# Products without a reader on TensorE, and the reversed scan's parts at other steps

## The reference, cut to what matters

```python
x = _L0_conv_ref(x, ...)             # bidirectional selective scan (Mamba) over 2 images of 256 x 48 x 48
x = x + _L1_conv_ref(_gn(x), ...)    # linear attention block
t = _to_tokens(x)
t = t + _L2_attn_ref(_ln_t(t), ...)  # softmax attention
t = t + _L2_ffn_ref(_ln_t(t), ...)   # graph-gated experts
t = t + _L3_attn_ref(_ln_t(t), ...)  # att = sigmoid((n q) n^T);  att n
t = t + _L3_ffn_ref(_ln_t(t), ...)   # routed experts
...
def step(h, xs):                     # the scan, once forward and once reversed
    d_t, B_t, C_t, u_t = xs
    h = jnp.exp(d_t[..., None] * A) * h + (d_t * u_t)[..., None] * B_t[:, None, :]
    return (h, jnp.einsum('bdn,bn->bd', h, C_t))
# y * silu(z), then out_proj;  _ln_t: (v - mean) / sqrt(var + eps) over the channels
```

## Time and profile before

| | |
|---|---|
| median of 3 runs | 5890.46 us (5889.35 to 5890.49) |
| the profiled execution: its own time, its span | 5906.89 us, 5905.1 us |
| mean granted TensorE clock | 0.917 |
| busy: PE, DVE, ACT, POOL | 4882.1, 3428.7, 2082.3, 2321.0 us |

### The profile page before, as it was taken

How to read it: one execution, slowest core, us unless ns; L and a number is a source line. 1 busy time by engine, 2 the same in 40 slices (tenths; PEclk the granted TensorE clock), 3 DMA queues, 4 the chain that set the end, 5 groups by cost and what they waited for, 6 DMA issues and landing times. The chain is left out here.

```text
span 5905.1 us, 54130 instructions
## 1 busy us (share of the span) xinstructions
PE 4882.1 (83%) x15186; PEld 2726.7 (46%) x15187; DVE 3428.7 (58%) x4954; ACT 2082.3 (35%) x3362; POOL 2321.0 (39%) x2102
## 2 busy tenths in 40 slices
PE   5877888987778886998997876473999899997797
PEld 3333333433333332554555554452555555555575
DVE  2999999999999997693862323574222200002113
ACT  2655666656666563322321111000222212212123
POOL 3888888888888885011120000182000000002102
PEclk7999999999999999999998888586999999995899
DMA  2444344334443342001000001100001000001233
GB/s 97 134 117 149 126 125 129 117 120 135 126 132 123 120 135 83 29 0 52 28 14 16 5 16 42 26 5 7 23 16 44 19 0 2 0 0 41 72 95 75
DMA packets 221102, 383.47 MB, mean 65 GB/s; under 512 B 35036, under 2 KB 208269, under 8 KB 216037
## 3 DMA queue, kind: packets, MB, share of 16 engines
q1 hardware_dynamic: 206868, 367.49, 19.6%
q0 software_dynamic: 7552, 7.81, 0.8%
q10 hardware_dynamic: 6480, 5.90, 0.4%
HBM read 334.99 MB, written 48.71 MB: 65 GB/s over the span
## 5 line engine op out<-in xcount | busy, mean ns | idle before, releaser
L917 POOL TENSOR_TENSOR DBU<-DU,BB 128x461 f32<-128x461 f32 (+1 forms) x1280 | 1371.4, 1085 | 330.6 <-DVE PS L961 320.1
L592 PE MATMUL PS<-G,ident 128*128 128x461 f32 (+1 forms) x2560 | 1158.3, 580 | 390.0 <-DVE G L972 388.0
L961 DVE TENSOR_TENSOR_SCAN PS<-PS,HC,DBU 128x461 f32<-128x461 f32 (+1 forms) x1024 | 1147.9, 1165 | 5.0 <-ACT PS L768 5.0
L768 ACT ACTIVATE PS<-DT,alog 128x461 f32<-128x461 f32 (+1 forms) x1280 | 825.8, 645 | 817.0 <-DVE PS L961 814.7
L592 PEld LDWEIGHTS PS<-G,ident 128*128 128x128 f32 x2560 | 462.1, 194 | 1051.5 <-DVE G L972 801.8
L972 DVE TENSOR_TENSOR G<-PS,CB 128x461 f32<-128x461 f32 (+1 forms) x1280 | 785.8, 623 | 38.7 <-PE PS L592 38.6
L2717 POOL TENSOR_TENSOR xs<-X 128x384 f32 x12 | 11.7, 991 | 829.7 <-issue 527.9
L2686 DVE TENSOR_TENSOR X<-X,PS 128x768 f32 x12 | 11.4, 954 | 553.5 <-PE PS L2653 553.5
L2581 DVE TENSOR_TENSOR Hg<-Hg,GB 128x384 f32<-128x384 f32 x192 | 106.7, 558 | 372.8 <-ACT Hg L2568 372.8
L2642 PE MATMUL PS<-QT,N 128*128 x864 | 310.3, 486 | 4.9 <-ACTq L2659 4.9
L2653 PE MATMUL PS<-AT,XT 128*128 128x384 f32 x864 | 310.5, 487 | 0.0
(11 more groups left out here) (423 smaller groups left out, 7515.8 us busy)
## 6 DMA issues: line engine op xcount, KB each, us to landing
BB<-proj_dram SPq DMA_DIRECT2D x256, 461.0 KB, 3.9
CB<-proj_dram SPq DMA_DIRECT2D x64, 922.0 KB, 6.1
BB<-proj_dram SPq DMA_DIRECT2D x64, 460.0 KB, 4.6
ew<-in_l_w SPq DMA_DIRECT2D x16, 1024.0 KB, 6.8
CB<-proj_dram SPq DMA_DIRECT2D x16, 920.0 KB, 5.9
GB<-gate_dram SPq DMA_DIRECT2D x12, 768.0 KB, 4.1
w_fc<-in_l_w_fc SPq DMA_DIRECT2D x4, 2048.0 KB, 11.8
XI<-xi_dram SPq DMA_DIRECT2D x8, 928.0 KB
```

The source lines that it names most:

```text
L592: pe.matmul(PS[:, j, :wide(g)], k.ident[:], G[:, S % 4, :wide(g)], start=False, stop=(n == DS - 1))\
L768: act.activation(DA(S), DT[:, j, :wide(g)], ACT.Exp, scale=w.alog[:, chunk(g)[1], j, n:n + 1]).then_inc(da_done, 1)
L917: pool.tensor_tensor(DBU[:, S % 4, :wide(g)], DU[:, j, :wide(g)], BB[:, 2 * u + n % 2, :wide(g)], ALU.mult).then_inc(dbu_done, 1)
L961: dve.tensor_tensor_scan(flow(HS(S), g), flow(DA(S), g), flow(DBU[:, S % 4, :wide(g)], g), start, ALU.mult, ALU.add).then_inc(h_done, 1)
```

## The change

It has two parts. First, a helper `spin` issues a product of the identity, repeated three times (384 columns), with `mean_w` into a piece of PSUM that nothing reads afterwards: two at each of the 8 steps of `norm_image`, one at each of 6 steps of `sigmoid_input`, one at each of 12 steps of `route_images`. That is 64 + 12 + 12 = 88 products. Second, in the scan other step numbers: `conv` one step later in every chunk; the four `out` parts from steps 22, 23, 25, 26 to 48, 49, 51, 52, into PSUM banks 0 and 1 in place of 2 and 3; `take_out` from 33 to 55; `z` from 47, 48, 53, 55 to 55, 56, 59, 61, and ACT's parts of z with it, `log_z` and `sig_z` now in steps 0 to 3 of the next chunk; `gate_z` on POOL from 1, 3, 6, 9 to 5, 7, 9, 11; `xi` beside a finished reversed chunk from 47, 48, 52, 53 to 55, 56, 59, 60.

```diff
+def spin(pe, k, dst, n):
+
+    wide = k.ident[:].rearrange("p (o n) -> p o n", o=1).broadcast_to([P, n, P])
+    pe.matmul(dst, k.mean_w[:], wide, start=True, stop=True)
...
                         pe.matmul(k.PS[:, s % DEEP, :T], k.mean_w[:], xs[:, s % DEEP, :], start=True, stop=True)\
                           .then_inc(mean_ready, 1)
+                    spin(pe, k, k.PS[:, 7, :T], TT)
                     if 1 <= s <= NT:
...
                         mm.then_inc(var_ready, 1)
+                    spin(pe, k, k.PS[:, 7, :T], TT)
                     if s >= 2:
...
-                    if s == 10:
+                    if s == 11:
                         conv(h, 0)
-                    elif s == 12:
+                    elif s == 13:
                         conv(h, 1)
-                    elif s == 15:
+                    elif s == 16:
                         conv(h, 2)
-                    elif s == 18:
+                    elif s == 19:
                         conv(h, 3)
...
                 if is_rev(g - 1):
-                    if s == 22:
+                    if s == 48:
                         out(g - 1, 0, 0)
-                    elif s == 23:
+                    elif s == 49:
                         out(g - 1, 0, 1)
-                    elif s == 25:
+                    elif s == 51:
                         out(g - 1, 1, 0)
-                    elif s == 26:
+                    elif s == 52:
                         out(g - 1, 1, 1)
...
-                    if s == 47:
+                    if s == 55:
                         z(h, 0)
-                    elif s == 48:
+                    elif s == 56:
                         z(h, 1)
-                    elif s == 53:
+                    elif s == 59:
                         z(h, 2)
-                    elif s == 55:
+                    elif s == 61:
                         z(h, 3)
...
-                if s == 33 and is_rev(g - 1):
+                if s == 55 and is_rev(g - 1):
                     take_out(g - 1)
...
                     if 1 <= s <= NT:
                         v = s - 1
-                        pe.wait_ge(sq_summed, v + 1)
                         if v >= 2:
                             pe.wait_ge(normalized, v - 1)
+                        spin(pe, k, k.PS[:, 2 + v % 2, P:P + T], TT)
+                        pe.wait_ge(sq_summed, v + 1)
```

More of the change, by code:

```diff
@@ L366, in mamba_chunks, with xi_at, xi_taken @@
     LATE = 2 * MC - 2
+    def xi_at(g):
+        if g == LATE:
+            return 62, 62, 63, 63
+        return (55, 56, 59, 60) if is_rev(g - 1) else (47, 48, 52, 53)
+    def xi_taken(g):
+        return (58, 59, 61, 62) if is_rev(g - 1) else (52, 53, 57, 58)
     with nc.Block() as block:
@@ L474, in xi @@
                     pe.wait_ge(dt_base, 2 * (h - 1) + 1)
+                    if h >= 2 and rev_before(h - 2):
+                        pe.wait_ge(o_added, rev_before(h - 2))
                     if is_rev(h - 1):
@@ L533, in z @@
                     pe.wait_ge(dt_base, 2 * h + 1)
+                    if rev_before(h - 1):
+                        pe.wait_ge(o_added, rev_before(h - 1))
                 else:
@@ L560, in first @@
                     pe.wait_ge(dt_base, 2 * g + 1)
+                    if g and rev_before(g - 1):
+                        pe.wait_ge(o_added, rev_before(g - 1))
                     if rev:
@@ L620, in _ @@
                 if is_rev(h):
-                    if s == 47:
+                    if s == 55:
                         z(h, 0)
-                    elif s == 48:
+                    elif s == 56:
                         z(h, 1)
-                    elif s == 53:
+                    elif s == 59:
                         z(h, 2)
-                    elif s == 55:
+                    elif s == 61:
                         z(h, 3)
[L629 to L637, removed]
+                if is_fwd(g + 2) and s in xi_at(g):
+                    for j in range(JD):
+                        if s == xi_at(g)[j]:
+                            xi(g + 2, j)
                 if s == STEPS - 1 and h < NCH:
@@ L743, in take_out @@
                 act.wait_ge(o_ready, rev_before(g) + 1)
-                act.activation(k.X[:, :, b * L + at:b * L + at + n], PS[:, 2:2 + KC, :n], ACT.Copy).then_inc(o_added, 1)
+                act.activation(k.X[:, :, b * L + at:b * L + at + n], PS[:, 0:KC, :n], ACT.Copy).then_inc(o_added, 1)
             act.preload_act_table_set("natural_log_exp_and_others")
@@ L810, in _ @@
                 if is_rev(h):
-                    if s == 52:
+                    if s == 58:
                         take_z(h, 0)
-                    elif s == 53:
+                    elif s == 59:
                         exp_z(h, 0)
-                    elif s == 54:
                         take_z(h, 1)
-                    elif s == 55:
+                    elif s == 60:
                         exp_z(h, 1)
-                    elif s == 56:
-                        log_z(h, 0)
-                    elif s == 57:
+                    elif s == 61:
                         take_z(h, 2)
-                    elif s == 58:
+                    elif s == 62:
                         exp_z(h, 2)
-                    elif s == 59:
+                    elif s == 63:
                         take_z(h, 3)
-                    elif s == 60:
                         exp_z(h, 3)
[L829 to L843, removed]
+                if is_rev(g):
+                    if s == 0:
+                        log_z(g, 0)
+                    elif s == 1:
+                        sig_z(g, 0)
+                    elif s == 2:
+                        log_z(g, 1)
+                    elif s == 3:
+                        sig_z(g, 1)
+                if is_fwd(g + 2) and g != LATE and s in xi_taken(g):
+                    take_xi(g + 2, xi_taken(g).index(s))
                 if g == LATE and s == 63:
@@ L917, in _ @@
                 pool.tensor_tensor(DBU[:, S % 4, :wide(g)], DU[:, j, :wide(g)], BB[:, 2 * u + n % 2, :wide(g)], ALU.mult).then_inc(dbu_done, 1)
-                if is_rev(g) and s in (1, 3, 6, 9):
-                    gate_z(g, (1, 3, 6, 9).index(s))
+                if is_rev(g) and s in (5, 7, 9, 11):
+                    gate_z(g, (5, 7, 9, 11).index(s))
                 if s == 14 or s == 16:
```

15 lines of the change are left out of this document (8 added, 7 removed).

## The result

The changed kernel takes 5917.4 us (median of 6 runs, 5909.6 to 5924.8) beside 5890.5 (6 runs, 5887.7 to 5900.0): a ratio of 1.0043, 95% interval 1.0031 to 1.0055. It is slower by about 26 us. The forecast was 5917 us, in a range of 5875 to 5945, with a chance of 0.65 for slower.

What follows compares the result with a forecast made beforehand. DVE was taken to bound the scan, and PE at the lower clock to be nearest the bound in norms, sigmoid inputs and routing. Scan +21, norms +5, inputs +3, routing -2 gave +27 us: median 5917, range 5875 to 5945.

Steps and rivals of the forecast that it cites:

- conv, -32 us: Scan: with conv one step later, DVE's mixes wait less for PE's accumulation, 14.3 + 24.3 - 6 = 32 us gained.
- take_out, 9 x 3.0 us: Scan: ACT's copy waits 5.1 us for out's last product, delaying scan 56 by 3.0 us in nine reversed chunks, +27 us.
- What follows, 26 us: Scan: ACT's later parts (floor_rest, z, xi) delay further decays after the late copy, 26 us, bounds 0 and 40.
- The scan: +21 forecast: Whole scan: the gain of 32 us against 53 us of stall and follow-ons, +21 us.
- The norms, +5 us: Four norm calls: two added products a step raise the clock but cost PE time, +5 us, bounds -10 and +79.
- The full steps: Norms, 20 steps with the pipeline full: 7 lose 0.4 us each, 13 win 0.5 each, +2.8 - 6.5.
- the ends: Norms, first and last steps, pipeline not full: nothing hides the added products, 4 x 2.2 = 8.8 us.
- Sigmoid inputs and routing, +3 and -2: Added products cost 9 and 7 us there, a higher clock returns 6 and 9: +3 and -2 us.
- The first: Rival, scan: out ends before about 884.6, so take_out does not stall; -14 us, 5876; chance 0.12.
- The second: Rival, routing and sigmoid inputs: 2.4 GHz from near their start, gains -28 and -6; about +8, 5898; chance 0.13.
- The third: Rival: products don't raise the clock; norms cost 79 us, sigmoid inputs 13, routing 7; +120, 6010; chance 0.06.

## Why the prediction was right

By its own steps:

**conv, -32 us.** Right in size for the change as a whole: the mixes' waits fell by 28.8 us (38.6 to 9.8). What is left is 6.4 us at step 40, behind xproj, as forecast, and 3.5 at step 20 in five chunks, where the prediction had acc(17) ready in time. The reason given was half of it. The step "the new steps 11, 13, 16, 19 put acc(13) and acc(19) ahead of conv" holds for the forward chunks, where the run with conv alone won 1.1 us each. Where an out stands beside them they go only if out is moved too, which the change did and the prediction did not name as a condition; with conv alone 25.6 us of waits stay. Not foreseen was that `take_conv` is then late for DA(25), which makes a pair 0.27 us longer in most chunks.

**take_out, 9 x 3.0 us.** Right. The wait of ACT was put at 5.1 us and is 5.20 to 5.22 in eight of the nine chunks (5.46 in chunk 10), the delay of scan 56 at 3.0 and the distance of the pairs is 3.06 us longer in eight of nine chunks (3.3 in chunk 10), together some 28 us. That its length is PE's work at 0.386 us a pass is shown by the run with four passes fewer. By an estimate from the Trainium skill's rule for the distance of products ("TensorE: Matmul & The Clock Gate", Back-to-back issue gap) the term would have been 0; the fp32 passes of this kernel keep 0.386 us, and the measurement decides.

**What follows, 26 us.** Right in sum, which the parts give as follows: the pair at 56 later by 0.37 (0.5 taken), the z parts by 0.75 + 0.43 + 0.36 = 1.54 a chunk (1.7 taken), the end of chunk 8 by 2.5 (1 taken), the chunks with xi about 2 each. The run with z alone shows 14.4 of them without out. The scan: +21 forecast, +24.4 in the trace.

**The norms, +5 us.** The step at 2.4 GHz is 3.27 us (3.35 taken), the clock 0.95, as forecast. In the five traces with two products against the five without, the start averages 97.3 and 96.5 us, the second norm 30.5 and 29.2, the third 28.3 and 29.7: together +0.7, not +5. The third norm's 1.4 us is a steady gain; the other places differ by as much between traces without a product. The full steps gave what was forecast: from the first to the fifth spread of each norm the four take 51.3 us together on average with the products and 55.6 without, -4.3 where I had 2.8 - 6.5 = -3.7. The term that was too large is the ends: put at 4 x 2.2 = 8.8, they come to 0.7 + 4.3 = 5.0.

**Sigmoid inputs and routing, +3 and -2.** The inputs differ by less than 1 us on average (57.7 with, 58.4 without; 51.0 and 51.2). The routing gains 5, 167.3 on average in the six traces with one product and 172.5 in the five without. On the whole it is shorter, in both groups, where its first 69 us have the higher clock: 173.8 us at 0.55 and about 171.5 at 0.61 without, 169.7 at 0.70 and 166.7 at 0.78 with one. So the clock gave more than I took, or the waits hid more of the products; how much each, no run here tells.

**The attentions, not in the sum.** No edit touches them, and they are 3 us longer in the trace of after. PE has no idle time in them (busy 260 of 260 us in a stretch of before), and their first 20 us differ in the clock. Here are those of the second attention in the traces of before, of after and of the 88 products alone:

```profile
5039.00:5059.00 20.00, 17.64 (x56) 10.29 (x55) 0.42 (x1) 4.70 (x9) 0.00 (x0) 1.00 0.00 0
5054.00:5074.00 20.00, 18.46 (x52) 10.83 (x53) 0.00 (x0) 4.72 (x8) 0.00 (x0) 0.91 0.00 0
5063.00:5083.00 20.00, 18.60 (x48) 10.76 (x49) 0.00 (x0) 4.72 (x8) 0.00 (x0) 0.83 0.00 0
```

From its first to its last product an attention takes 279.2 us where that clock is 1.00, 280.8 at 0.91 and 282.1 at about 0.84, in all 24 attentions of the twelve traces. With one product in the inputs both start below 1.00 (561.5 to 563.0 us together), with none at most the second does (558.4 to 560.0), with two neither (558.3). So one product in the inputs also cost the attentions 1.5 to 4.6 us, which the prediction had at nothing.

**The sum.** That the median came out at 5917.4 where 5917 was forecast is luck to that degree. Between the two traces the scan is 3.4 us over its term, the norms at +3.1 are 2 under theirs, the inputs and the routing at -3.8 are 5 under, the attentions are 3 over; these cancel. The medians of before in the later groups, 5891.7 to 5925.0 us, show how far a median moves by itself.

**The rivals.** The first (no stall at `take_out`) is refuted by its wait of 5.20 us; it needed the end of out before 884.6 in the trace of before, and the block ran in the time counted. The second was right that the clock rises: 0.87 in the sigmoid input, 0.70 in the routing. Its gains of 28 and 6 us are not there; the routing gained 5 and the inputs less than 1. The third is refuted by the clock.

## What to carry to other kernels

A copy on an in-order engine that waits for a block of another engine's work belongs as many steps behind that block as the block takes beyond the steps it spans; count the passes of the block and what must run beside it, and compare with the step. Moving a part of a packed in-order queue by one step is judged with its neighbours, not alone: conv alone won 7.5 us, and with out one or two steps later 33. Products that only keep the clock up cost their own time once PE is at the higher clock: add as many as fit into PE's idle time there. One a step was best in these norms (the third took 25.7 us, 28.3 with two and 29.7 with none) and in the routing (167.3 us, 169.1 with three and 172.5 with none); in the sigmoid inputs one won less than 1 us and cost more than that in the attention behind them.

## What was not expected of the hardware

A few us at the lower clock at the start of a stage in which PE is never idle lengthen it by nearly the same amount each time: the attentions take 279.2, 280.8 or 282.1 us and nothing between. And a stage with small transfers and gathers, untouched by any edit, varied by 40 us between traces (425 to 465 us), with single waits of 20.8 and 21.8 us on transfers (`proj_dram<-PJ` and the gather `RD<-dst_dram,IX`); that is more than the effect of most edits here, and only stage lengths in the traces made these readable.
